# Delta rule on raw keys: one factor per source token, the second key turn dropped, and the key-key product put in that turn's place in TensorE's list

## What is computed

```
q, k, v = silu(causal_conv1d(x @ w_qkv, conv_w))          # 4 taps
q = q * rsqrt(sum(q*q) + eps);  k = k * rsqrt(sum(k*k) + eps)
for t in tokens:
    St = St * exp(g_t)
    delta = (v_t - k_t @ St) * beta_t
    St = St + outer(k_t, delta)
    o_t = (q_t * 128**-0.5) @ St
core = rmsnorm(o) * norm_weight * silu(x @ w_z);  out = core @ w_out
```

## Time and profile before

| what | value |
|---|---|
| median of three runs | 3313.22 us |
| profiled execution, its span | 3310.8 us, 60236 instructions |
| TensorE matmuls (PE) | 3215.4 us busy, 97% |
| TensorE weight loads (PEld) | 2131.6 us, 64% |
| VectorE (DVE) | 2448.0 us, 74% |
| ScalarE (ACT) | 1550.6 us, 47% |
| GpSimd (POOL) | 1859.5 us, 56% |

### The profile page before, as it was taken

The page is one execution under the profiler, slowest core; times in us unless marked ns, Lnnn a source line. Parts: engine busy times, 40 slices in busy tenths (PEclk is TensorE's granted clock), DMA queues, the critical chain, the costliest instruction groups (busy, mean ns, idle before and its releaser), DMA issues. The chain is left out here.

```text
span 3310.8 us, 60236 instructions
## 1 busy us (share of the span) xinstructions
PE 3215.4 (97%) x20576; PEld 2131.6 (64%) x20576; DVE 2448.0 (74%) x3686; ACT 1550.6 (47%) x4983; POOL 1859.5 (56%) x1824
## 2 busy tenths in 40 slices
PE   5899999999999999999999999999979999999999
PEld 2577777777777777777777777777754444454444
DVE  6899999999999999999999999999940011034453
ACT  2465656565656565556555655565531000022232
POOL 2677777777777777777777777777730000011132
PEclk8999999999999999999999999999999999999999
DMA  2133333323333233323333332333325222211001
GB/s 94 48 77 84 77 72 74 85 70 74 80 84 75 69 80 76 77 70 83 80 75 73 80 81 70 77 79 81 81 62 207 76 102 102 76 39 64 0 13 39
DMA packets 423119, 248.75 MB, mean 75 GB/s; under 512 B 306688, under 2 KB 372352, under 8 KB 417280
## 3 DMA queue, kind: packets, MB, share of 16 engines
q1 hardware_dynamic: 421520, 237.81, 27.5%
q10 hardware_dynamic: 1296, 7.08, 0.5%
HBM read 156.39 MB, written 71.57 MB: 69 GB/s over the span
## 5 line engine op out<-in xcount | busy, mean ns | idle before, releaser
L736 PE MATMUL acc<-xT,wc 128*128 128x512 f32 x2048 | 934.8, 599 | 2.7 <-PEq L112 2.0
L736 PEld LDWEIGHTS acc<-xT,wc 128*128 128x128 f32 x2048 | 369.7, 190 | 372.6 <-issue 372.0
L1015 DVE SCALAR_TENSOR_TENSOR d_conv<-acc,wc,d_conv 128x511 f32<-128x511 f32 (+2 forms) x768 | 566.8, 738 | 41.8 <-ACT d_conv L1190 32.6
L749 PE MATMUL acc<-wc,xT 128*128 128x256 f32 x2048 | 473.4, 384 | 0.0
L749 PEld LDWEIGHTS acc<-wc,xT 128*128 128x128 f32 x2048 | 379.1, 190 | 46.2
L1541 PE MATMUL acc<-t_area 128*128 128x512 f32 x768 | 332.5, 592 | 1.6 <-ACT t_area L1990 1.6
L634 POOL TENSOR_TENSOR d_bf<-d_kks,d_gam 128x512 f32<-128x512 f32 x128 | 160.6, 1277 | 294.9 <-ACT d_kks L1234 294.9
L2047 POOL TENSOR_SCALAR t_veps<-t_mv 128x1 f32<-128x1 f32 x32 | 9.7, 303 | 547.0 <-DVE t_mv L1786 547.0
L1048 DVE STREAM_TRANSPOSE d_em<-d_dm 128x1024 f16<-128x1024 f16 x256 | 314.5, 1228 | 2.2
L1776 DVE TENSOR_TENSOR t_x<-acc,t_x 128x512 f32<-128x512 f32 x16 | 11.1, 691 | 392.3 <-PE acc L1541 392.3
L1055 DVE TENSOR_TENSOR d_zm<-d_tz,cons 128x512 f16<-128x512 f32 x384 | 259.0, 674 | 52.0 <-PE d_tz L799 47.0
(11 more groups left out here) (228 smaller groups left out, 7002.3 us busy)
## 6 DMA issues: line engine op xcount, KB each, us to landing
d_decay<-decay_rows SPq DMA_DIRECT2D x64, 512.0 KB, 5.2
v_rows<-d_vb SPq DMA_DIRECT2D x256, 128.0 KB, 2.3
d_vn<-v_rows SPq DMA_DIRECT2D x64, 512.0 KB, 3.7
core_rows<-d_ob SPq DMA_DIRECT2D x1024, 32.0 KB, 1.7
t_area<-core_rows SPq DMA_DIRECT2D x30, 1024.0 KB, 4.8
wc<-in_w SPq DMA_DIRECT2D x96, 256.0 KB, 3.2
d_qn<-d_qf SPq DMA_DIRECT2D x1024, 16.0 KB, 1.8
t_x<-in_x SPq DMA_DIRECT2D x4, 1024.0 KB, 9.2
```

Source lines behind the costliest of these rows:

```text
L736: last = nc.tensor.matmul(bank(TILE[j])[:, :], wtile(j, k), xT[:, k, r % B * S:(r % B + 1) * S], start=k == 0, stop=k == KT - 1)
L749: last = nc.tensor.matmul(bank(f"z{j}")[:, i * GV * P:(i + 1) * GV * P].rearrange("p (h n) -> p h n", h=GV), xT[:, k, r % B * S + (2 * j + ...
L1015: nc.vector.scalar_tensor_tensor(c[:, d:S], bank(TILE[j])[:, 0:S - d], tap(j, KS - 1 - d), c[:, d:S], ALU.mult, ALU.add).then_inc(taps, 1)
```

## The change

Raw keys are used throughout. kT is the SiLU output itself; the factor per source token j is applied where a token is a partition: kk and kq are copied out in four chunks, each scaled by 1/(sum k_j^2 + eps), khat becomes k_j times that, and the values are multiplied by sqrt(sum k_j^2 + eps), in four new operations on ScalarE. The power on GpSimd now makes both factors (8 numbers in place of 4), in two buffers. The second turn with its copy is gone, and kk stands in its place in TensorE's list.

```diff
@@ k_norm (GpSimd)
-                wait(pool, khat_ready, at(back(n, 1), NC, NC))
-                nc.gpsimd.tensor_tensor(rk[:, :], rkt[:, :], cons[:, C_POW:C_POW + NC], ALU.pow).then_inc(rk_ready, 1)
+                wait(pool, kqs_ready, at(back(n, 2), NC, NC))
+                wait(pool, v_scaled, at(back(n, 2), NC, NC))
+                nc.gpsimd.tensor_tensor(rk[n[1] % 2][:, :, :], bc(rkt[:, :], 2), cons[:, C_KPOW:C_KPOW + 2 * NC].rearrange("p (e c) -> p e c", e=2),
+                                        ALU.pow).then_inc(rk_ready, 1)
...
@@ TensorE
-                turn(bank("k_turn"), kraw, k_turned)
-
-            def khat_turn(n):
-                pe.wait_ge(khat_ready, at(n, NC, NC))
-                ring_free(n, "khat_turn")
-                turn(bank("khat_turn"), khat[n[1] % 2], khat_turned)
+                turn(bank("k_turn"), kT[third(n)], k_turned)
...
             def kk(n):
-                pe.wait_ge(kT_ready, count(n))
+                pe.wait_ge(silued, nth(n, "silued", 0))
...
@@ solve(s, 0)
-                    pe.wait_ge(v_moved, at(s, 80, 80))
+                    pe.wait_ge(v_scaled, at(s, NC, NC))
...
@@ TensorE's list
                 if invert:
                     level_d(m, 2)
                 if project:
-                    khat_turn(n)
+                    kk(n)
                 if recur:
                     solve(s, 1)
                     head_start(s, 2)
...
                     grow(s, 1)
                     head_start(s, 4)
-                if project:
-                    kk(n)
                 if invert:
                     level_d(m, 3)
...
@@ silu (ScalarE)
-                    wait(act, k_turned, count(n, 1))
+                    wait(act, ks_s, at(back(n, 3), 3, 3))
...
-                out = (kraw[:, :], qT[third(n)][:, :], v[:, 0, :], v[:, 1, :])[j]
+                out = (kT[third(n)][:, :], qT[third(n)][:, :], v[:, 0, :], v[:, 1, :])[j]
...
-            def copy_kT(n):
-                act.wait_ge(khat_turned, count(n))
-                nc.scalar.activation(kT[third(n)][:, :], bank("khat_turn")[:, :], ACT.Copy).then_inc(kT_ready, 1)
+            def scale_v(s):
+                act.wait_ge(v_moved, at(s, 80, 80))
+                for c in range(NC):
+                    v = vn[s[1] % 2][:, :, :, :].rearrange("p a (h c) j -> p (a h) c j", c=NC)[:, :, c, :]
+                    nc.scalar.activation(v, v, ACT.Copy, scale=rk[s[1] % 2][:, 1, c:c + 1]).then_inc(v_scaled, 1)
...
-                nc.scalar.activation(kks[:, :], bank("kk")[:, :], ACT.Copy).then_inc(kk_copied, 1)
+                for c in range(NC):
+                    nc.scalar.activation(chunk(kks, c), chunk(bank("kk"), c), ACT.Copy, scale=rk[n[1] % 2][:, 0, c:c + 1]).then_inc(kk_copied, 1)
...
-                nc.scalar.activation(kqs[:, :], bank("kq")[:, :], ACT.Copy).then_inc(kqs_ready, 1)
+                for c in range(NC):
+                    nc.scalar.activation(chunk(kqs, c), chunk(bank("kq"), c), ACT.Copy, scale=rk[m[1] % 2][:, 0, c:c + 1]).then_inc(kqs_ready, 1)
...
@@ ScalarE's list
                     o_square(f, 0, 1)
                     read_q(f, 2, 0)
                 if recur:
+                    scale_v(s)
                     copy_d(s, 5, 0)
...
-                if project:
-                    copy_kT(n)
```

More of the change, by code:

```diff
@@ L45 @@
 C_RMS = C_L2 + NC
-C_END = C_RMS + NC
+C_KPOW = C_RMS + NC
+C_END = C_KPOW + 2 * NC
 DECW = S
@@ L68, in shape_constants @@
     c[:, C_RMS:C_RMS + NC] = L2_EPS * RMS_EPS * HD
+    c[:, C_KPOW:C_KPOW + NC] = -1.0
+    c[:, C_KPOW + NC:C_KPOW + 2 * NC] = 0.5
     for h in range(XH):
@@ L323, in delta_rule @@
         cb, decay, ident = many("conv", 2, [P, S]), sb("decay", [P, GV, S]), sb("ident", [P, S])
-        kraw, vraw, vn = sb("kraw", [P, S]), sb("vraw", [P, GV, S]), many("vn", 2, [P, NC, GV * NC, 32])
+        vraw, vn = sb("vraw", [P, GV, S]), many("vn", 2, [P, NC, GV * NC, 32])
         khat = many("khat", 2, [P, S])
@@ L340, in delta_rule @@
         junk, kqs, kks = sb("junk", [P, 3 * NC, P], BF16), sb("kqs", [P, S]), sb("kks", [P, S])
-        kss, qss, rkt, rk = sb("kss", [P, NC]), sb("qss", [P, NC]), sb("rkt", [P, NC]), sb("rk", [P, NC])
+        kss, qss, rkt, rk = sb("kss", [P, NC]), sb("qss", [P, NC]), sb("rkt", [P, NC]), many("rk", 2, [P, 2, NC])
         qf, qn = sb("qf", [P, NC, NC, 32]), sb("qn", [P, NC, NC, 32])
@@ L354, in delta_rule @@
         k_turned, k_squares, rk_ready = sem("k_turned"), sem("k_squares"), sem("rk_ready")
-        khat_ready, khat_turned, kT_ready, ks_ready = sem("khat_ready"), sem("khat_turned"), sem("kT_ready"), sem("ks_ready")
+        khat_ready, ks_ready, v_scaled = sem("khat_ready"), sem("ks_ready"), sem("v_scaled")
         q_moved, q_squares, eq_ready = sem("q_moved"), sem("q_squares"), sem("eq_ready")
@@ L430, in per_token @@
             return bc(ap, P, 2)
-        RING_ORDER = ("q", "k", "z1", "v1", "k_turn", "z0", "kq", "v0", "khat_turn", "kk")
-        RING_BANK = {"q": 1, "k": 2, "z1": 0, "v1": 1, "k_turn": 2, "z0": 0, "kq": 2, "v0": 0, "khat_turn": 2, "kk": 1}
+        RING_ORDER = ("q", "k", "z1", "v1", "k_turn", "z0", "kq", "v0", "kk")
+        RING_BANK = {"q": 1, "k": 2, "z1": 0, "v1": 1, "k_turn": 2, "z0": 0, "kq": 2, "v0": 0, "kk": 1}
         RING_FREED = {"k": (taps, "taps", 2), "q": (taps, "taps", 5), "v0": (taps, "taps", 8), "v1": (taps, "taps", 11),
                       "z0": (z_silued, "z_silued", 0), "z1": (z_silued, "z_silued", 1),
-                      "k_turn": (khat_ready, "squares", NC - 1), "khat_turn": (kT_ready, "once", 0),
-                      "kk": (kk_copied, "once", 0), "kq": (kqs_ready, "once", 0)}
+                      "k_turn": (khat_ready, "squares", NC - 1),
+                      "kk": (kk_copied, "squares", NC - 1), "kq": (kqs_ready, "squares", NC - 1)}
         CONV_ORDER = ("k", "v1", "v0", "q")
@@ L448, in delta_rule @@
                     "zr_ready": (1, 2), "closed": (2, 1), "tt_ready": (2, 1)}
-        RING_LAG = {"q": 1, "k": 0, "z1": 2, "v1": 0, "k_turn": 0, "z0": 2, "kq": 1, "v0": 0, "khat_turn": 0, "kk": 0}
+        RING_LAG = {"q": 1, "k": 0, "z1": 2, "v1": 0, "k_turn": 0, "z0": 2, "kq": 1, "v0": 0, "kk": 0}
         CONV_LAG = {"k": 0, "v1": 0, "v0": 0, "q": 0}
@@ L630, in b_full @@
             def b_full(n, h):
-                pool.wait_ge(kk_copied, count(n))
+                pool.wait_ge(kk_copied, at(n, NC, NC))
                 pool.wait_ge(gams_ready, nth(n, "gams_ready", h))
@@ L636, in p_full @@
             def p_full(m, h):
-                pool.wait_ge(kqs_ready, count(m))
+                pool.wait_ge(kqs_ready, at(m, NC, NC))
                 pool.wait_ge(gamc_ready, nth(m, "gamc_ready", h))
@@ L779, in kq @@
             def kq(m):
-                pe.wait_ge(kT_ready, count(m))
                 pe.wait_ge(silued, nth(m, "silued", 1))
@@ L1246, in normal_k @@
                 for c in range(NC):
-                    nc.scalar.activation(chunk(khat[n[1] % 2], c), chunk(bank("k_turn"), c), ACT.Copy, scale=rk[:, c:c + 1]).then_inc(khat_ready, 1)
+                    nc.scalar.activation(chunk(khat[n[1] % 2], c), chunk(bank("k_turn"), c), ACT.Copy, scale=rk[n[1] % 2][:, 0, c:c + 1]).then_inc(khat_ready, 1)
             def copy_kq(m):
```

## The result

The changed kernel takes 3339.35 us (median of 4 runs, 3338.90 to 3340.12) against 3313.93 for the kernel before on the same chip: ratio 1.0079, 95% interval 1.0065 to 1.0093. The change makes the kernel slower by 25 us. The forecast was 3339, with "slower" at 0.88.

A forecast was written before the change was run, and what follows sets the result against it. Two chains from level_d(m, 2) to read_k(s, 2) were taken to bound the kernel, VectorE's the later. Slot shift 11.2, refine's stall 15.8 and first slots -1 made 26 us: 3313.2 + 26 = 3339, range 3322 to 3354.

The forecast's parts named there:

- What bounds the kernel: From level_d(m, 2) to read_k(s, 2): TensorE's and VectorE's chains arrive together, VectorE's the later; removing TensorE work alone gains nothing.
- kk in the turn's place: Slot end: kk delays level_z(m, 3), VectorE's mask and state, hence read_k(s, 2), by 0.18 us; 62 slots, 11.2 us.
- the f16-to-fp32 term of 0.08: kk's new place behind an fp16 step: its fp32 products take 0.08 us longer, 0.97 instead of 0.89.
- The scalings: Weight-loading slots: four v scalings ahead of copy_d, 0.37 us each, make refine wait 1.05 us; 15 times, 16 us.
- First slots: First two slots: TensorE waits for the key's chain, so the dropped turn and copy save at most 2 us, taken as 1.
- Quarter copies, the longer power, the new waits: ScalarE's scaled quarters of kk and kq, GpSimd's power at 1.64 instead of 1.01 us, added waits: all covered, costing nothing.
- The sum: Whole run: 11.2 + 15.8 - 1 = 26 us on the median, 3313.2 + 26 = 3339.
- A: Rival: waits at read_k only apparent, TensorE's list decides, the dropped turn pays in full: -13, 3300 us; chance 0.07.
- B: Rival: only one loss occurs, the slot shift alone (3324) or the refine stall alone (3328); chance 0.10.
- C: Rival: no change, shift zero and stall small as tap weights come earlier against TensorE; 3313 within 6; chance 0.05.
- E: Rival: each v scaling costs over 0.55 us, showing in ordinary slots too; at 0.65, 3376 us; chance 0.03.
- D: Rival: waits at attend and refine lower the granted clock in 15 weight-loading slots: 51 us more, 3390; chance 0.04.

The follow-up runs named there:

- the run with both edits: The changed kernel with kk put back behind grow(s, 1) and the scalings of v put behind copy_d(s, 5, 0): 3313.26 us, ratio 1.0002.
- the fastest order: Changed kernel, kk behind grow, v scalings behind copy_d, last two tile(n, 2) matmuls behind solve(s, 1), residual(s, 1) ahead of flip_o: 3275.96 us, ratio 0.9886.

## Why the prediction was right, point by point

*What bounds the kernel.* Right, and shown: the added VectorE copy is paid one for one, and the turn is worth nothing with kk in its old place. The sign that gave it away was a weight load that starts with its product; it is gone where the turn was made twice. (One slip in the reading: `level_d(m, 2)` ends 0.40 from its start, at 1540.45 on the trace's clock; the prediction's "0.40 + 0.05" mixes the two. Nothing hangs on it.)

*kk in the turn's place, 0.18 us a slot, 11.2 us.* Right in mechanism, the size was 0.23 a slot, 14 us. Every TensorE start up to `grow` was within 0.01 us, the f16-to-fp32 term of 0.08 included (kk lasted 0.98, taken as 0.97). The missing 0.05 is mostly on VectorE: the mask, which now waits for its input, takes 0.69, not 0.65; the state starts 0.61 behind it, not 0.58, and its two halves take 0.60, not 0.58.

*The scalings, 1.05 us in 15 slots, 16 us.* Right in place and count. A scaling took 0.40 us from start to start ((1.70 - 0.50) / 3) where I took 0.37, so `refine` lost 1.16. But the term is net 0.8 (1.04 less the 0.23 of every slot), 12 us, and the prediction added it in full, saying that nothing had slack: `attend`'s wait had (6.2 us in 15 waits), and shrank to 1.6 in 2 because TensorE came later. With the fixed cost of about 93 ns that the Trainium skill (Perfetto Trace Analysis, "Optimizing Scalar/DVE Operations") gives, the estimate for a scaling was 0.25; the measurement is 0.40 and decides.

*First slots, -1 us.* Wrong: the first three became 1.1 us longer. The first interval did shrink, from 21.2 to 19.9 us, but the next grew from 34.3 to 36.5. In it the granted clock was at its lower level (0.50) for 12.8 us, where it was so for 6.8 in the kernel before; ahead of the second drop TensorE had stood 1.43 us for VectorE's mask, with kk already done (0.33 in the kernel before, behind kk). With kk back behind grow the interval takes 35.0 us, with 6.8 of them at the lower level; with the scalings alone moved it takes 36.5. So some 1.4 of the 2.3 us go with kk's place; how much of that is the clock and how much the waiting is not shown.

*Quarter copies, the longer power, the new waits: nothing.* Right, shown together by the run with both edits.

*The sum.* 11.2 + 15.8 - 1 was to be 26, and between the profiled executions it is 14.0 (0.234 over the 60 slots behind the first three) + 12.1 + 1.1 = 27.2. The three terms are off by +2.8, -3.7 and +2.1; that the total is nearer than its parts is luck.

*The rivals.* A (TensorE's list decides) is out for the changed kernel, with kk in either place; it holds for work added to the kernel before and for the fastest order. B is out: each loss goes with its own edit. C is out, though part of its condition came true in `attend`'s shorter wait. E is out, the scaling costs 0.40. D did not happen in the changed kernel's profiled execution: the granted clock was 1.00 in every slot behind the first two intervals, here an ordinary and a weight-loading one (the column after POOL):

```profile
1545.69:1582.45 36.76, 36.40 (x283) 26.43 (x279) 34.47 (x52) 24.01 (x84) 27.39 (x27) 1.00 0.35 79
1507.65:1545.69 38.04, 36.68 (x282) 26.40 (x279) 33.84 (x52) 24.00 (x84) 26.70 (x27) 1.00 0.35 84
```

But D was no empty rival. With kk back behind grow, one of the 15 weight-loading slots took 40.58 us, 2.2 more than the others: TensorE stood 1.06 us ahead of `attend` (0.42 to 0.63 in the others) and 1.00 ahead of `refine`, and 0.4 us after `refine` began the granted clock was 0.50 for 3.4 us. One slot of the changed kernel had waits of 1.0 and 1.0 there and no such drop, so that the two waits bring it is not shown.

## What to carry to other kernels

Where two engines hand work to and fro, find the points at which their chains part and meet, and time both chains between them: a removed step pays only on the longer one and only down to the shorter, while an added or moved step can cost on either. Work that follows the last input of a chain is its cover; before moving it ahead of that input, ask what will stand in the gap. And put an added operation behind the one that others wait for in the slot in which its engine is latest, not where the average slot has room.

## What the runs showed of the hardware

- A semaphore wait that is only just met shows in no list of waits: in the kernel before, `read_k(s, 2)` came 0.05 us later than TensorE's list alone would have had it (3.55 against 3.50), and the list has one such wait of 0.3 us in the whole run; yet 0.13 us more in that chain cost 6 us. The weight load's start against its product's shows it: together where the state is awaited, 0.03 us ahead of it where it isn't.
- From the end of VectorE's state to the start of `read_k`, where TensorE waits for it: 0.053 to 0.057 us in every slot of both kernels.
- fp32 products behind an fp16 step take longer than behind fp32 ones: kk 0.97 to 0.98 us from start to start against 0.89.
- ScalarE on fp32 in SBUF with a factor per partition, from start to start: 128x128 in 0.29 us, 128x256 in 0.40.
- The same VectorE mask has no single time: 0.65 us right behind the flip, 0.68 behind the added copy, 0.69 where it had waited for its input.
